# One period of an attention loop: norm, transposes, u and the LayerNorm pipeline in another order of queues

## The reference

```python
x = x + L0(gn(x), ...)          # gn: each channel of an image normalised over its 32 x 32 places
def L0(z):                      # N = 16 images, H = 8 heads of C = 16
    zn = (z - mean) * rsqrt(var + eps) * ln_w + ln_b      # over the channels
    q, k, v = zn @ Wq, zn @ Wk, zn @ Wv
    g = sigmoid(zn @ Wg + bg)
    att = softmax over image j of q[i].k[j] / 4           # per place and head: 16 x 16
    o = (att @ v) * g
    return o @ Wo + bo
x = x + L1(gn(x), ...)          # a gated triangle product, the second stage
```

## Time and profile before

| what | value |
|---|---|
| median of 3 runs | 340.28 us (339.03 to 341.97) |
| the profiled execution's own time | 342.18 us |
| its span in the profile | 340.2 us |
| TensorE matmul busy | 247.4 us (73%) |
| VectorE busy | 250.9 us (74%) |
| ScalarE busy | 215.8 us (63%) |
| GpSimd busy | 196.5 us (58%) |
| mean granted TensorE clock | 0.946 of full |

### The profile page before, as it was taken

The page is one execution under the profiler, slowest core; times in us unless marked ns, Lnnn a source line. Parts: engine busy times, 40 slices in busy tenths (PEclk is TensorE's granted clock), DMA queues, the critical chain, the costliest instruction groups (busy, mean ns, idle before and its releaser), DMA issues.

```text
span 340.2 us, 7453 instructions
## 1 busy us (share of the span) xinstructions
PE 247.4 (73%) x2978; PEld 145.4 (43%) x2982; DVE 250.9 (74%) x463; ACT 215.8 (63%) x392; POOL 196.5 (58%) x172
## 2 busy tenths in 40 slices
PE   0066965579789689689689689675774499998734
PEld 0045442357346346346346346344350245554233
DVE  4985879796798898898898895899646753441872
ACT  4634788289569579579679669567170366558612
POOL 6890474479886987977978944237271583000520
PEclk9999999698999999999999999999599599999977
DMA  7100213013031031031021023100000004666407
GB/s 249 35 0 0 63 55 75 0 40 87 0 94 33 2 94 36 17 79 33 32 63 35 31 64 71 25 0 3 0 4 0 1 5 98 176 169 178 120 0 247
DMA packets 34893, 19.66 MB, mean 58 GB/s; under 512 B 21228, under 2 KB 31788, under 8 KB 34860
## 3 DMA queue, kind: packets, MB, share of 16 engines
q1 hardware_dynamic: 34860, 19.20, 21.0%
HBM read 8.71 MB, written 6.29 MB: 44 GB/s over the span
## 4 chain that ended last, share of the span: by engine, by line
DVE 40%; PE 40%; ACT 11%; issue 6%; DMA 1%; DVEq 0%; POOL 0%
PE PS L1128 35%; DVE nmax L899 5%; DVE t_sb L883 5%; DVE S_sb L903 5%; DVE og L876 4%; DVE gn_part L966 3%; DVE sums L827 3%; ACT PP L631 2%; PE PS L1197 2%; DVE Z L1115 2%; PE PS L1393 2%; DVE rden L845 1%; ACT t_sb L615 1%; DVE Z L1119 1%; ACT S_sb L621 1%
## 5 line engine op out<-in xcount | busy, mean ns | idle before, releaser
L1128 PE MATMUL PS<-znT,A_bd 128*128 128x512 f16 x192 | 47.0, 386 | 11.3 <-DVE t_sb L883 10.1
L428 POOL TENSOR_TENSOR S_sb<-S_sb,rden 128x512 f32<-128x512 f32 x32 | 35.5, 1133 | 27.6 <-DVE rden L845 27.6
L883 DVE TENSOR_TENSOR t_sb<-PS,t_sb 128x512 f16<-128x512 f32 x64 | 41.2, 684 | 9.2 <-ACT t_sb L615 8.7
L615 ACT CAST t_sb<-PS 128x512 f16<-128x512 f32 x64 | 36.6, 618 | 13.8 <-PE PS L1128 12.5
L621 ACT ACTIVATE S_sb<-S_sb 128x512 f32<-128x512 f32 x32 | 20.3, 634 | 31.7 <-DVE S_sb L903 31.7
L434 POOL TENSOR_TENSOR PP<-S_sb,PP 128x512 f16<-128x512 f32 x28 | 31.8, 1158 | 9.5 <-ACT PP L609 9.5
L1128 PE MATMUL PS<-zbd,t_sb 128*128 128x64 f16 x768 | 27.7, 196 | 12.9 <-DVE t_sb L883 12.2
L1128 PEld LDWEIGHTS PS<-zbd,t_sb 128*128 128x128 f16 x768 | 24.9, 100 | 24.0 <-DVE t_sb L883 16.5
L1128 PEld LDWEIGHTS PS<-znT,A_bd 128*128 128x128 f16 x192 | 16.7, 98 | 39.9 <-DVE t_sb L883 23.8
L411 POOL TENSOR_TENSOR ln_rs<-ln_ve,minus_half 128x16 f32<-128x16 f32 x7 | 20.4, 2914 | 23.0 <-DVE ln_ve L822 23.0
L601 ACT COPY u_sb<-PS 128x512 f32<-128x512 f32 x64 | 33.1, 642 | 0.2 <-PE PS L1128 0.2
(11 more groups left out here) (198 smaller groups left out, 532.7 us busy)
## 6 DMA issues: line engine op xcount, KB each, us to landing
Z<-zn_dram SPq DMA_DIRECT2D x64, 64.0 KB, 2.9
x_tok<-in_x SPq DMA_DIRECT2D x4, 512.0 KB, 5.8
zn_dram<-zn_tok SPq DMA_DIRECT2D x8, 256.0 KB, 2.0
zbd<-znT SPq DMA_DIRECT2D x32, 64.0 KB, 2.0
k_dram<-og SPq DMA_DIRECT2D x4, 512.0 KB, 3.5
th<-k_dram SPq DMA_DIRECT2D x16, 128.0 KB, 2.7
out_x<-u_sb SPq DMA_DIRECT2D x4, 512.0 KB, 3.3
PP<-u_sb SPq DMA_DIRECT2D x8, 128.0 KB, 2.4
```

The costliest lines, as they stand in the source:

```text
L428: nc.gpsimd.tensor_tensor(P, P, bcast(rden[:, 32 * k:32 * k + 32], 2, N), ALU.mult).then_inc(p_nrm, 1)
L615: nc.scalar.copy(t_sb[:, HI, :, h], bank_tg(h)[:, :].rearrange("p (q i) -> p q i", i=N)).then_inc(t_hi, 1)
L883: nc.vector.tensor_tensor(t_sb[:, LO, :, h], bank_tg(h)[:, :].rearrange("p (q i) -> p q i", i=N), t_sb[:, HI, :, h], ALU.subtract).then_in ...
L1128: return nc.tensor.matmul(o, l, r, start=start, stop=stop)
```

## The change

- P's transposes (`pe_PT`) and their copies belong to period j = m + 1, the one in which P is normalised: blocks 0 and 1 stand after t and before the first scores, blocks 2 and 3 after the scores of block 2. VectorE copies block 0 before the first maximum and block 2 after the third subtraction; ScalarE copies block 1 after `p_high` and block 3 after the second exp.
- TensorE's period starts with u, in two halves of four parts with zn's transposes between them. Parts 1 and 2 wait for the subtractions of the period before (banks 3 and 4).
- All sums and reciprocals stand near the start of VectorE's period, each sum over two blocks (128x1024). x1 moves from the end of a period to the start of the next.
- ln_w and ln_b are no longer applied to the stream. They are folded into A_bd, the gate's weights and bias, a bias `t_bias` of t and the scale and bias of the u copies. A few small matrix products and operations in the prologue prepare this; one more small load is made.
- Centring and square go from VectorE and ScalarE to GpSimd; VectorE keeps the mean (`dve_ln_mean`, a reduce and a scaling) as its period's first instruction. GpSimd's two front steps move to the end of its period, behind the low part of zn. ScalarE's high part of zn moves behind gates 2 and 3.

The diff, cut to its core:

```diff
-            sp.dma_start(b_bc[:, :], ln_b.partition_broadcast(128)).then_inc(wts_in, 16)
+            for v, w in ((w_col, ln_w), (b_col, ln_b)):
+                sp.dma_start(v[:, :], w.unsqueeze(0).to_broadcast([A2, D]).unsqueeze(2)).then_inc(wts_in, 16)
...
-        def pool_ln_back(pool, j, par):
+        def pool_ln_centre(pool, j, par):
             zf = zc[:, par].rearrange("p e b d -> p (e b) d")
+            pool.wait_ge(ln_v, LV * j + 2)
+            nc.gpsimd.tensor_tensor(zf, zf, bcast(ln_mu[:, par], 2, D), ALU.subtract).then_inc(ln_z, 1)
+        def pool_ln_rstd(pool, j, par):
             pool.wait_ge(ln_v, LV * (j + 1))
             nc.gpsimd.tensor_tensor(ln_rs[:, par], ln_ve[:, par], minus_half[:, 0:A2 * SB], ALU.pow).then_inc(ln_z, 1)
-            pool.wait_ge(ln_z, LZ * (j - 1) + 3)
+        def pool_ln_scale(pool, j, par):
+            zf = zc[:, par].rearrange("p e b d -> p (e b) d")
+            pool.wait_ge(ln_z, LZ * (j - 1) + 4)
             nc.gpsimd.tensor_tensor(zf, zf, bcast(ln_rs[:, par], 2, D), ALU.mult).then_inc(ln_z, 1)
-            pool.wait_ge(ln_z, LZ * (j - 1) + 4)
-            nc.gpsimd.tensor_tensor(zf, zf, bcast(w_bc[:, :], 1, A2 * SB), ALU.mult).then_inc(ln_z, 1)
-            pool.wait_ge(ln_z, LZ * (j - 1) + 5)
-            nc.gpsimd.tensor_tensor(zf, zf, bcast(b_bc[:, :], 1, A2 * SB), ALU.add).then_inc(ln_z, 1)
...
+        def pool_ln_square(pool, j, par):
+            zf = zc[:, par].rearrange("p e b d -> p (e b d)")
+            pool.wait_ge(ln_z, LZ * (j - 1) + 3)
+            nc.gpsimd.tensor_tensor(sq[:, 0:512], zf, zf, ALU.mult).then_inc(ln_q, 1)
         def pool_period(pool, j, par, tail=True, LN=True, stats=True):
             if LN and not (j == 0):
-                pool_ln_front(pool, j + 1, 1 - par)
+                pool_ln_centre(pool, j + 1, 1 - par)
+            if stats:
+                pool_sqx(pool, j - 3)
+            if LN and not (j == 0):
+                pool_ln_square(pool, j + 1, 1 - par)
             if tail:
                 pool_norm(pool, j - 1, (0, 1))
-            if stats:
-                pool_sqx(pool, j - 3)
-            if tail:
                 pool_norm(pool, j - 1, (2, 3))
-            if LN:
-                pool_ln_back(pool, j + 1, 1 - par)
             own = tail and not (j == 1)
             if own:
                 p_low(pool, nc.gpsimd, j - 1, (0, 1))
             if LN:
-                pool_ln_low(pool, j + 1, 1 - par)
+                pool_ln_rstd(pool, j + 1, 1 - par)
             if own:
                 p_low(pool, nc.gpsimd, j - 1, (2, 3))
+            if LN:
+                pool_ln_scale(pool, j + 1, 1 - par)
+                pool_ln_low(pool, j + 1, 1 - par)
+            if LN and not (j == NS - 2):
+                pool_ln_front(pool, j + 2, par)
...
-                    nc.scalar.copy(u_sb[:, :, 4 * k:4 * k + 4].rearrange("p h q i -> p q h i"),
-                                   bank_u(k)[:, :].rearrange("p (q h i) -> p q h i", q=4, h=H)).then_inc(u_ok, 1)
+                    nc.scalar.activation(u_sb[:, :, 4 * k:4 * k + 4].rearrange("p h q i -> p q h i"),
+                                         bank_u(k)[:, :].rearrange("p (q h i) -> p q h i", q=4, h=H), ACT.Identity,
+                                         bias=b_col[:, :], scale=w_col[:, :]).then_inc(u_ok, 1)
...
-                    nc.scalar.copy(t_sb[:, HI, :, h], bank_tg(h)[:, :].rearrange("p (q i) -> p q i", i=N)).then_inc(t_hi, 1)
+                    nc.scalar.activation(t_sb[:, HI, :, h], bank_tg(h)[:, :].rearrange("p (q i) -> p q i", i=N),
+                                         ACT.Identity, bias=t_bias[:, h:h + 1]).then_inc(t_hi, 1)
...
             if B:
-                PT_copy(1)
+                u_copies(range(4))
             if A and not early:
                 act_znT(act, j)
-            if B:
-                PT_copy(3)
-                u_copies(range(4))
-            if LN and not early:
-                act_ln_square(act, j + 1, 1 - par)
             if B:
                 u_copies(range(4, 8))
...
+                    PT_copy(1)
                 exps((0,))
                 gates((0, 1))
                 exps((1,))
+                if j == 1:
+                    PT_copy(3)
                 gates((2, 3))
...
                 p_high((0, 1, 2) if A else range(4))
             if A:
                 t_high(range(3, H))
-            if LN:
-                act_ln_high(act, j + 1, 1 - par, half + par)
-            if tail and A:
-                p_high((3,))
+            if tail:
+                if A:
+                    p_high((3,))
+                PT_copy(1)
             if A:
                 exps((0,))
                 gates((0, 1))
                 exps((1,))
-                gates((2,))
+            if tail:
+                PT_copy(3)
+            if A:
+                gates((2, 3))
+            if LN:
+                act_ln_high(act, j + 1, 1 - par, half + par)
+            if A:
                 exps((2, 3))
-                gates((3,))
...
+        def dve_ln_mean(dve, j, par):
+            dve.wait_ge(ln_z, LZ * (j - 1) + 2)
+            nc.vector.tensor_reduce(ln_mu[:, par], zc[:, par].rearrange("p e b d -> p (e b) d"), op=ALU.add,
+                                    axis=AX.X).then_inc(ln_v, 1)
+            dve.wait_ge(ln_v, LV * j + 1)
+            nc.vector.tensor_scalar(ln_mu[:, par], ln_mu[:, par], 1.0 / D, None, ALU.mult).then_inc(ln_v, 1)
...
+        def dve_sums(dve, m, half):
+            dve.wait_ge(s_exp, 4 * m + 2 * half + 2)
+            nc.vector.tensor_reduce(sums[:, 64 * half:64 * half + 64], S_sb[:, 16 * half:16 * half + 16]
+                                    .rearrange("p q a n -> p (q a) n"), op=ALU.add, axis=AX.X).then_inc(p_sum, 1)
...
-            for i, k in enumerate((0, 2)):
-                if B:
-                    dve.wait_ge(pt_mm, 4 * s + k + 1)
-                    nc.vector.tensor_copy(PT[:, 8 * k:8 * k + 8].rearrange("p q m -> p (q m)"),
-                                          bank_b(k)[:, :].bitcast(f16)).then_inc(pt_ok[0], 1)
-                if tail:
-                    dve_sums(dve, m, (2 + i,))
...
+            if LN and not (j == 0):
+                dve_ln_mean(dve, j + 1, 1 - par)
+            if stats:
+                dve_x1(dve, s - 1)
             if tail:
-                dve_reciprocal(dve, m, 1)
-            if LN and not (j < 2):
-                dve_ln_centre(dve, j + 1, 1 - par)
-                dve_ln_rstd(dve, j + 1, 1 - par)
+                for half in range(2):
+                    dve_sums(dve, m, half)
+                    dve_reciprocal(dve, m, half)
             if stats:
...
+            if LN and not (j == 0):
+                dve_ln_rstd(dve, j + 1, 1 - par)
...
+                nc.vector.scalar_tensor_tensor(out=t_sb[:, LO, :, h],
+                                               in0=bank_tg(h)[:, :].rearrange("p (q i) -> p q i", i=N),
+                                               scalar=t_bias[:, h:h + 1], in1=t_sb[:, HI, :, h], op0=ALU.add,
+                                               op1=ALU.subtract).then_inc(t_lo, 1)
...
-                if j == 1:
-                    if h == 3:
-                        dve_ln_centre(dve, 2, 0)
-                    if h == 5:
-                        dve_ln_rstd(dve, 2, 0)
-                    if h in (2, 4):
-                        p_low(dve, nc.vector, 0, (h - 2, h - 1))
+                if j == 1 and h in (2, 4):
+                    p_low(dve, nc.vector, 0, (h - 2, h - 1))
             if B and not A:
                 gate_o(range(A2))
+            if tail:
+                PT_copy(0)
...
-                if k in (1, 2):
-                    dve_sums(dve, j, (k - 1,))
-                if k == 2:
-                    dve_reciprocal(dve, j, 0)
-            if B:
...
+                if k == 2 and tail:
+                    PT_copy(2)
+            if tail and not A:
+                PT_copy(2)
...
+        def pe_u(pe, s, par, half, ks):
+            if ks[0] == 0:
+                pe.wait_ge(Z_ld[par], 128 * (half + 1))
+            for k in ks:
+                if k in (1, 2) and s < NS - 1:
+                    pe.wait_ge(s_sub, 4 * (s + 1) + k + 2)
...
+                if j == 1:
+                    pe_PT(pe, m, (0, 1))
...
-            pe_PT(pe, s, (0, 1))
+            pe_u(pe, s, par, half, range(4))
             if A:
                 pe_znT(pe, j, par)
-            pe_PT(pe, s, (2, 3))
-            pe_u(pe, s, par, half)
+            pe_u(pe, s, par, half, range(4, 8))
             if not A:
                 pe_o(pe, s)
+                if m < NS:
+                    pe_PT(pe, m, range(4))
                 pe_out(pe, s)
                 return
             pe_t(pe, j, (0, 1, 2))
             pe_o(pe, s)
             pe_t(pe, j, range(3, H))
+            pe_PT(pe, m, (0, 1))
             pe_scores(pe, j, (0, 1))
             pe_gate(pe, j, (0, 1))
             pe_scores(pe, j, (2,))
```

(39 more changed lines are left out.)

105 lines of the change are left out of this document (57 added, 48 removed).

## The result

The changed kernel takes 360.35 us (median of 4 runs, 357.85 to 362.97), the kernel before 341.12 us beside it (4 runs): a ratio of 1.059, 95% interval 1.054 to 1.064. That is 19.2 us slower, where 350.0 was forecast and the range ended at 359. The profiled execution took 359.42, its span is 357.6.

A forecast was written before the change was run, and what follows sets the result against it. The prediction took the hand-over between VectorE and TensorE, neither full, as the bound. Span 340.2 + 6.1 for periods and ends + 3.6 for the clock = 349.9, own time 351.9, 1.9 above the median: 350.0, range 337 to 359.

The forecast's parts named there:

- (b): TensorE's queue: P's transposes of blocks 0 and 1 hide in a 1.40 us wait; u runs right after the out projection.
- (c): Steady period: GpSimd's next block comes late, VectorE idles 4.4 us before the mean; 26.85 instead of 25.14 us, +1.71.
- (e): TensorE's clock: a 3.8 us lull in four periods, a shorter one in period 2; three falls at 1.2 us, +3.6.
- falls in every lull: Rival: clock falls in every TensorE lull (5 x 2.8), or sums at their slow end; 357 to 360 us, chance 0.15.
- (d): Sum over stretches: four full periods +6.8, period 2 -0.6, period 7 -1.5, start +1.1, drain +0.3; +6.1 us.
- (a): Work per period: VectorE about 0.7 us less, ScalarE 1.6 more from per-partition operands, GpSimd about even.
- faster rival: Next block reaches VectorE in time, ScalarE's u copies bind every period: 24.0 us each, 334.6 in all, chance 0.13.

The follow-up runs named there:

- e4: Changed kernel with 16 matmuls whose result nobody reads filling TensorE's wait before zn's transposes in periods 2 to 6: 353.78 us, ratio 1.040.
- e1: Changed kernel with GpSimd's two front steps of the next block ahead of zn's low part instead of behind it: 339.61 us, ratio 0.998.
- e9: Changed kernel with ScalarE's high part of zn ahead of the copy of P's block 3 and gates 2 and 3: 347.81 us, ratio 1.020.
- e2: Changed kernel with VectorE's mean behind x1, sums and reciprocals, GpSimd's order kept: 349.95 us, ratio 1.028.
- e6: e1 with all folding undone: GpSimd applies ln_w and ln_b in two more passes a period, copies plain: 330.02 us, ratio 0.966.
- e8: Kernel before with scale 1 and bias 0 in u copies, bias 0 in t copies, scalar 0 in t residuals: 351.75 us, ratio 1.034.
- e5: e1 with plain u and t copies and t residuals, leaving out ln_w and ln_b of v and t's bias: 325.56 us, ratio 0.956.
- e7: Changed kernel with plain u and t copies and t residuals, leaving out the same parts as e5: 352.43 us, ratio 1.035.

## Why the prediction was wrong

The sign and the mechanism were right, the size was not: the clock, the two ends and the sum of a period were each put too low. Both profiles can be set side by side by stretches between the scores. Before: to S of period 1, 65.15; period 2, 26.27; four full periods, 100.55; period 7, 25.49; from there to the second stage, 44.06. In microseconds after minus before:

| stretch | forecast | after | e4 (no fall in the periods) |
|---|---|---|---|
| up to the scores of period 1 | +1.1 | +2.9 | +1.8 |
| period 2 | -0.6 | -1.0 | -1.0 |
| four full periods | +6.8, and +3.6 for the clock | +14.65 | +9.1 |
| period 7 | -1.5 | -1.35 | -1.35 |
| drain | +0.3 | +2.1 | +1.6 |
| second stage | 0 | +0.1 | +1.2 |
| sum | +9.7 | +17.4 | +11.3 |

Of the 7.7 us that were missing, 3.9 are the clock's (5.55 in the four periods and 1.9 at the ends, for 3.6), 2.3 the sum's of the four periods, and 1.6 the rest of the two ends; the other rows nearly cancel.

**(b) was right.** P's transposes cost nothing: in the steady rows TensorE waits neither for the copies of P nor for the subtractions, and out ends and u follows as worked out (u 0 to 3 from S+7.55, against S+7.85 for the end of out).

**(c), the mechanism, was right to a few tenths.** High part S+6.67 (forecast S+6.7), idle before the mean 4.87 (4.4), lull of TensorE 4.34 (3.8), a long sum 1.21 (1.24 with its gap). That the order does it is shown by e1, which moves two instructions and gives back all of the loss. **The sum failed by 0.6 a period**: 27.4 with the lull filled (e4), 26.85 forecast. The fronts end 0.2 later, as the high part takes 1.37 beside other work where I took 1.07 of the earlier trace rows and the low part 1.47. The scaling of the variance took 0.41 (the row of 169.50), where that of the mean, of the same form, took 0.17. These make the larger part of it; the rest is spread over terms of a tenth. Over four periods it is 2.3 (9.1 for 6.8).

**(e), the clock, failed most.** I took three falls at 1.2 us, 3.6. The windows show a fall in all four full periods, two of them at 0.88, and half clock right behind the lull. In the four periods they cost 5.55 (115.20 to 109.65 from scores to scores, after and e4), by period 0.6, 1.9, 0.9 and 2.1, or 1.4 on average. Both factors of the term failed, the three falls and the 1.2 for each, and so did the reason for them, that u, t and o have 0.46 to spare behind the lull: u at half clock used that up, and in the period from 121.34 VectorE waited 1.02 for the first copy of t (141.61) and 0.74 for o (144.41). The rival "falls in every lull" had the number of falls nearly right (it counted five with period 2, whose lull ahead of the transposes was only 0.92 and brought none); it had 0.15. That its time, 357 to 360, lies next to the measured one is luck: it priced a fall at 2.8, twice what was measured, and had neither the longer sum of (c) nor the longer ends.

The last two windows of the first table start 1 us or less behind the end of a lull: TensorE is busy all the time, at half clock, which is 1.2 GHz. The Trainium skill ("TensorE: Matmul & The Clock Gate", section "HAM oscillation — how this bites in real kernels") says that a loop with a recurring wait pays the cold start on every burst. The traces agree for lulls of 4.3 us, four times in four; for lulls of 2.2 us they agree two times in four in e9 and two times in four in e2. The kernel before had none in its steady periods, whose longest lull is 1.4. I had cited the rule and weighed the dense work behind the lull against it; that argument was wrong.

**(d) failed by 3.6, 1.8 at each end,** and 1.9 of it is the clock again. The same two stretches of the kernel before, by windows:

```profile
44.56:65.15 20.59, 11.80 (x140) 5.98 (x141) 18.50 (x30) 15.61 (x30) 9.61 (x9) 0.91 0.21 53
217.46:261.52 44.06, 31.49 (x452) 18.16 (x452) 32.82 (x69) 20.69 (x35) 20.46 (x16) 0.92 0.01 2
```

After, the clock is 0.84 and 0.82 in them. At the first end 1.1 is the clock's (21.42 against e4's 20.30 with the same instructions). The other loss is the start: the first scores come at 46.61 instead of 44.56, 2.05 later. In the five kernels with the whole folding they come at 46.55 to 46.64, in e6, which folds nothing, at 44.82, so most of this is the price of the folding before the first scores. The forecast had +1.1 for the whole of this end.

In the drain the rows tell the parts. Before:

```profile
247.32 3.87 PE L1128 MATMUL PS<-PP,Z 128*128 128x128 f16 x64
...
252.50 2.35 PE L1128 MATMUL PS<-u_sb,Wv_p 32*32 32x512 f32 x64 [1.32 <-ACT u_sb L601]
```

After:

```profile
257.26 2.92 PE L1233 MATMUL PS<-ident,PP 128*128 128x128 f16 x24 [6.99 <-DVE og L892]
...
262.81 4.15 PE L1164 MATMUL PS<-PP,Z 128*128 128x128 f16 x64
...
269.00 3.17 PE L1164 MATMUL PS<-u_sb,Wv_p 32*32 32x512 f32 x64 [2.04 <-ACT u_sb L621]
```

From the scores of period 7 to the last u it is 30.15 us after (232.66 to 262.81) and 29.86 before (217.46 to 247.32), so +0.3. The forecast let gains, the earlier transposing of the last P among them, pay for most of the copies. That transposing paid nothing: the transposes waited 6.99 for the gating on VectorE. From the last u to its o it is 6.19 against 5.18: the eight copies of u took 5.46 instead of 4.02, +1.0 where +1.5 was forecast. The last o took 3.17 instead of 2.35, +0.8, and that is the clock (in e4 it took 2.35). From the start of the out projection on nothing changed (5.91 and 5.88).

**(a) was wrong in a way that the total hid.** I took the folding as free but for +1.6 us of ScalarE, most of it covered, and a small +0.4 on VectorE. The durations were right (u copy 0.78, t copy 0.687 in the median where I had 0.68), the cover was not: on the kernel before the same operands cost 3.4%, 11.6 us (e8), in the new order without the stall 14.1 (e5 against e1), and with the stall still 7.9 (e7), nearly all of it outside the periods with the stall. In the forecast kernel the cover held where the mean was late; it failed at the start and in the drain. The 64 u copies of the changed kernel in the view by line (min, median, max in ns, first and last start):

```profile
L621 ACT ACTIVATE u_sb<-PS,b_col,w_col x64: 760/780/864, 76.7 to 268.1; 128x512 f32<-128x512 f32 x64
```

The same view gives 587, 643 and 692 ns for them before.

**The faster rival** had its turning point nearly right and its price wrong. It put that point at S+10.2 for the end of GpSimd's second step; in e9 the step ends at S+10.07 (129.65 and 1.28, from 120.86) and a period at full clock takes 25.3, just above the 25.14 of the kernel before. For a block that arrives in time it put 24.0 us a period and 334.6 us in all, though its terms add up to -5.3 and not to -6, which gives 335.0. e1 has that period (24.13) and takes 339.6, because the ends give back what the periods gain: its first stretch is 2.9 us longer than before, its drain 3.0 (47.09 against 44.06) and its second stage 1.0. The profiled execution of e1 took 341.53, 1.9 more than the median, so a part of these ends belongs to that execution.

What stays open is why the clock fell in two of e9's four equal lulls and in two of e2's, and not in the others. In e9 the periods alternate (0.94 and 1.00), as they do in the changed kernel (0.94 and 0.88). A wait of 2.23 in period 2 brought a fall in e9 (90.28) and none in the changed kernel (90.27), though TensorE's rows ahead of it agree to 0.05 us.

## What to carry to other kernels

Before work is moved to an engine with spare time, follow that engine's queue: an instruction that waits for another engine holds everything behind it, and here the two steps that began the next block stood behind such a one and cost 20.7 us, which putting them ahead gave back. A stall of TensorE can cost twice in such a loop, once for the wait and once for the clock behind it; filling the lull with useless matmuls measures the second part, if it is read in the periods that were filled and not from the total. And an operand that makes each copy 0.1 us dearer isn't free because its engine is a quarter idle. Where the copies stand in the chain from one product to the next they cost (1.84 us a period in e8); where another engine holds that chain up they hardly do (0.24 under the stall). Two whole passes a period on an engine off that chain were 9.6 us cheaper (e6 against e1).

## What the hardware showed

16 matmuls of 128x512 that nobody reads, 3.6 us of them in each lull, made the four full periods 5.55 us shorter (e4), with the granted clock at 1.00 in every one of them. On ScalarE the copies of t took 0.586 us plain and 0.687 with one operand per partition, those of u 0.643 plain and 0.780 with two; on VectorE the residual of t took 0.682 plain and 0.743 with one (medians of 64, before and after). The high part of zn, the same conversion of 128x512 from fp32 to fp16 on ScalarE, took 1.07 (before), 1.09 (e9), 1.37 (after) or 1.44 us (e4), and the scaling of the mean, 128x16 on VectorE, between 0.17 (after) and 0.88 us (e6, the row below, from its timeline). The quick ones ran while GpSimd stood idle; the slow one ran beside GpSimd's low part (122.14 to 123.62) and ended with it. The scaling of the variance, which runs beside GpSimd's normalising of P, took 0.385 in the median after. That GpSimd's work causes it was not tried. The length of such operations is not to be taken from a single row.

```profile
122.77 0.88 DVE L837 TENSOR_SCALAR ln_mu<-ln_mu 128x16 f32<-128x16 f32 x1
```
